# A small hybrid model on one core: the second layer's ternary maps, weight parts and softplus made inside the layer ahead of it

## What is computed

```python
# chosen-token layer: 128 tokens of highest score go through attention and a gated MLP
x1 = x + attn_out
h2 = rms_norm(x1, ln2_w)
mlp = silu(h2 @ w_gate) * (h2 @ w_up) @ w_down
...
# layer 1, gated recurrence along the tokens
gates, values = split(x @ W.T + b)
hidden = scan(sigmoid(gates), tanh(values))
...
# layer 1, ternary feed-forward (three maps of 1024 x 256)
scale = mean(abs(w)) + 1e-8
q = clip(round(w / scale), -1, 1) * scale
...
# layer 1, recurrent block
log_a = -8.0 * softplus(a_param) * sigmoid(x @ ga_W + ga_b)
```

## Time and profile before

| | |
|---|---|
| median of three runs | 1559.47 us (1554.13 to 1560.02) |
| the profiled execution, its time | 1559.31 us |
| its span | 1558.1 us |
| busy in the span | PE 94%, DVE 74%, ACT 66%, POOL 44% |
| TensorE's mean granted clock | 0.978 of full |
| f2: start, its `x1`, first addition to x | 1186.2, 1256.12, 1271.04 us |
| layer 1: first centring to the end | 1275.43 to 1558.1 us |

### The profile page before, as it was taken

The page is one execution under the profiler, slowest core; times in us unless marked ns, Lnnn a source line. Parts: engine busy times, 40 slices in busy tenths (PEclk is TensorE's granted clock), DMA queues, the critical chain, the costliest instruction groups (busy, mean ns, idle before and its releaser), DMA issues.

```text
span 1558.1 us, 23609 instructions
## 1 busy us (share of the span) xinstructions
PE 1461.4 (94%) x8358; PEld 1214.0 (78%) x8358; DVE 1145.6 (74%) x2617; ACT 1024.1 (66%) x2254; POOL 679.4 (44%) x802
## 2 busy tenths in 40 slices
PE   6999999999999998998999999999999987978898
PEld 4878888888888886686888888888886864655576
DVE  6888898989898985656675766766666748787646
ACT  3798989888888986453664655655654446464654
POOL 4557676665666554043433332333221411722233
PEclk8999999999999999998999999999999998998999
DMA  2000000000000000601000000000004122000000
GB/s 85 11 1 1 18 1 18 1 18 2 17 8 1 8 1 1 258 1 49 21 21 8 21 28 8 28 21 15 1 8 179 80 85 105 1 0 0 1 1 28
DMA packets 14341, 45.12 MB, mean 29 GB/s; under 512 B 3216, under 2 KB 3216, under 8 KB 12048
## 3 DMA queue, kind: packets, MB, share of 16 engines
q1 hardware_dynamic: 14224, 43.61, 7.9%
HBM read 42.55 MB, written 1.05 MB: 28 GB/s over the span
## 4 chain that ended last, share of the span: by engine, by line
PE 64%; DVE 16%; ACT 16%; issue 3%; POOL 1%; DMA 1%; SPq 0%; DVEq 0%; ACTq 0%; POOLq 0%
PE ps L148 26%; PE ps L345 13%; PE ps L1137 8%; PE ps L334 7%; ACT a_pT_hi L393 4%; ACT a_prob L361 3%; ACT a_o_two L634 3%; PE ps L1911 2%; DVE a_prob L354 2%; PE ps L1917 2%; DVE a_pT_lo L401 2%; ACT a_q L624 1%; DVE f_r L1527 1%; PE ps L1927 1%; PE ps L1913 1%
## 5 line engine op out<-in xcount | busy, mean ns | idle before, releaser
L376 POOL TENSOR_SCALAR a_prob<-a_prob,a_rowinv 128x128 f32<-128x128 f32 (+7 forms) x256 | 188.3, 750 | 164.2 <-DVE a_rowinv L370 164.2
L361 ACT ACTIVATE a_prob<-a_prob,a_negmax 128x128 f32<-128x128 f32 (+7 forms) x256 | 198.4, 780 | 32.5 <-DVE a_negmax L354 30.9
L401 DVE TENSOR_TENSOR a_pT_lo<-ps,a_pT_hi 128x512 fp32r<-128x512 f32 (+3 forms) x384 | 193.0, 549 | 19.9 <-ACT a_pT_hi L393 17.3
L376 POOL TENSOR_SCALAR b_prob<-b_prob,b_rowinv 128x128 f32<-128x128 f32 (+7 forms) x128 | 94.2, 748 | 234.6 <-DVE b_rowinv L370 234.6
L354 DVE CUSTOM_DVE_ANT_0 a_prob<-ps,a_mask 128x128 f32<-128x128 f32 (+7 forms) x256 | 187.2, 749 | 8.8 <-PE ps L148 8.4
L393 ACT ACTIVATE a_pT_hi<-ps 128x512 fp32r<-128x512 f32 (+3 forms) x384 | 164.2, 492 | 22.5 <-PE ps L334 9.9
L334 PE MATMUL ps<-ident,a_prob 128*128 128x128 f32 x1152 | 155.0, 275 | 8.8 <-DVE a_pT_lo L401 6.6
L361 ACT ACTIVATE b_prob<-b_prob,b_negmax 128x128 f32<-128x128 f32 (+7 forms) x128 | 99.7, 779 | 82.5 <-DVE b_negmax L354 82.3
L334 PEld LDWEIGHTS ps<-ident,a_prob 128*128 128x128 f32 x1152 | 128.9, 140 | 27.3 <-issue 11.2
L148 PE MATMUL ps<-a_k_hi,a_q 128*128 128x512 f32 (+3 forms) x384 | 141.0, 373 | 7.6 <-DVE a_negmax L354 7.5
L345 PE MATMUL ps<-a_pT_hi,a_v 128*128 128x512 f32 (+3 forms) x384 | 132.5, 352 | 1.6 <-DVE a_q L664 0.7
(11 more groups left out here) (449 smaller groups left out, 4145.1 us busy)
## 6 DMA issues: line engine op xcount, KB each, us to landing
f_wq<-in_f_wq SPq DMA_DIRECT2D x2, 2048.0 KB, 9.2
f_wo<-in_f_wo SPq DMA_DIRECT2D x2, 2048.0 KB, 17.5
b_w_raw<-in_b_qk SPq DMA_DIRECT2D x16, 256.0 KB, 2.6
a_w_raw<-in_a_w SPq DMA_DIRECT2D x8, 384.0 KB, 3.3
a_o_raw<-in_a_o SPq DMA_DIRECT2D x8, 256.0 KB, 2.7
f_wk<-in_f_wk SPq DMA_DIRECT2D x2, 1024.0 KB, 11.1
f_wv<-in_f_wv SPq DMA_DIRECT2D x2, 1024.0 KB, 13.1
f_wg<-in_f_wg SPq DMA_DIRECT2D x2, 1024.0 KB, 19.6
```

The costliest lines, as they stand in the source:

```text
L361: act.activation(prob, prob, ACT.Exp, bias=a.negmax[:, n:n + 1], scale=-1.0, accum_out=a.rowsum[:, n:n + 1]).then_inc(*g.exped.mark(a.tag, u))
L376: pool.tensor_scalar(prob, prob, a.rowinv[:, n:n + 1], 1.0, ALU.mult, ALU.mult).then_inc(*g.normed.mark(a.tag, u))
L401: dve.tensor_tensor(lo, src, fr(hi), ALU.subtract).then_inc(*g.lo.mark(a.tag, u, j0 // 4))
```

## The change

- In the layer f2 (`early=True`), layer 1's memory is laid out first, and tiles of `ffn` are put in another order, so that layer 1's early tiles lie on tiles of f2 that are dead by then (the rotary table, wq, wk, wv and two small masks).
- SP, at the end of f2's own loads, waits for `take` 7 and issues four small loads, then waits for the last query/key product and issues the three ternary weights and the recurrence's weights (`early_sp`). Layer 1's own list keeps the recurrent block's weights alone.
- The sum of absolute values moves from ACT to DVE (`early_abs_dve`, one `tensor_reduce` of 2048 columns), reading the same average matrix as the norms, with the factor 1/1024 in the scale. The three means on PE, the scales, five of the six half maps and the sixth in layer 1's first DVE step (`prep_dve`), the first half of the softplus and its Abs, Exp and Ln are put between f2's instructions. After the Ln ACT calls the root once (`warm_act`).
- POOL splits the recurrence's weights in f2, ahead of `ch` (`early_pool`).
- The four strings are written anew, for lists without most zeros. On POOL, the splits of layer 1's other weights stand at other places between the ring's low parts.

```diff
 def ffn_pool(g, f, pool):
...
             pool.tensor_tensor(g.x[:, k, cc], g.x[:, k, cc], f.h[:, k, cc], ALU.add).then_inc(*done.mark(tag, "x_plus", b, k))
+    if f.early:
+        early_pool(g, f.early, tag, pool)
     pool.wait_ge(*g.f_dve.at(tag, "x1"))
...
 def ffn_pe(g, f, pe):
...
     weigh(0)
+    if f.early:
+        early_pe(g, f.early, pe, 0, 3)
     turn_prob(2)
...
     weigh(3)
+    if f.early:
+        early_pe(g, f.early, pe, 1, 3)
     out(2)
...
     t.then_inc(*done.mark(tag, "chT"))
+    if f.early:
+        early_pe(g, f.early, pe, 2, 0)
     pe.wait_ge(*act.at(tag, "chT"))
...
 def ffn_act(g, f, act):
...
     weighed(2)
+    if f.early:
+        early_exp_act(g, f.early, act)
     weighed(3)
...
     act.activation(f.chT[:], bank[3][:, 0:D], ACT.Copy, scale=f.gate[:]).then_inc(*done.mark(tag, "chT"))
+    if f.early:
+        early_ln_act(g, f.early, act)
...
 def ffn_dve(g, f, dve):
...
     divide(2)
+    if f.early:
+        early_abs_dve(g, f.early, tag, dve, 0)
     divide(3)
+    if f.early:
+        dve.wait_ge(*pe.at(tag, "v", 1))
+        early_scale_dve(g, f.early, dve, 0, 3)
+        ternary_dve(g, f.early, dve, 0, 0)
+        early_abs_dve(g, f.early, tag, dve, 1)
+        ternary_dve(g, f.early, dve, 0, 1)
+        early_scale_dve(g, f.early, dve, 1, 3)
+        early_exp_dve(g, f.early, dve)
+        ternary_dve(g, f.early, dve, 1, 0)
     dve.wait_ge(*act.at(tag, "xs"))
     dve.wait_ge(*pe.at(tag, "wo"))
...
         dve.tensor_scalar(f.h2[:, k], f.x1[:, k], f.ln[:, 1, k:k + 1], None, ALU.mult).then_inc(*done.mark(tag, "h2", k))
+    if f.early:
+        ternary_dve(g, f.early, dve, 1, 1)
     dve.wait_ge(*act.at(tag, "root"))
...
+    if f.early:
+        early_abs_dve(g, f.early, tag, dve, 2)
+        early_scale_dve(g, f.early, dve, 2, 0)
+        ternary_dve(g, f.early, dve, 2, 0)
     for c, cc in halves():
         for m in range(KT):
             dve.wait_ge(*pe.at(tag, "put", m, c))
...
+def early_sp(g, l, tag, sp):
+    sp.wait_ge(*g.f_dve.at(tag, "take", TT - 1))
+    sp.dma_start(l.r_b[:], g.ins["r_b"]).then_inc(*g.r_loaded.mark("b", by=16))
...
+    sp.wait_ge(*g.f_pe.at(tag, "qk", len(F_ORDER) - 1))
+    for name, _, _ in TERNARY:
+        sp.dma_start(l.raw["t", name][:], g.ins["t_" + name]).then_inc(*g.t_loaded[name].mark(by=16))
+    sp.dma_start(l.raw_r[:], g.ins["r_w"]).then_inc(*g.r_loaded.mark("w", by=16))
+
+def early_pe(g, l, pe, n, bank):
+    pe.wait_ge(*g.prep_dve.at("abs", n))
+    pe.matmul(g.bank[bank][:, P + n * 32:P + n * 32 + 1], g.avg[:], l.part[:, n:n + 1], start=True, stop=True).then_inc(*g.prep_pe.mark("mean", n))
+
+def early_pool(g, l, tag, pool):
+    pool.wait_ge(*g.r_loaded.at("w"))
+    pool.wait_ge(*g.f_pe.at(tag, "v", 1))
+    split_in_place(pool, l.r_w, l.raw_r, g.prep_pool, "r")
+
+def early_abs_dve(g, l, tag, dve, n):
...
+    dve.tensor_reduce(l.part[:, n:n + 1], l.raw["t", name][:].rearrange(FLAT), AX.X, ALU.add,
+                      apply_absolute_value=True).then_inc(*g.prep_dve.mark("abs", n))
+
+def ternary_dve(g, l, dve, n, c):
...
+    dve.tensor_scalar(l.below[:, cc], raw[:, cc], s[:, 2:3], None, ALU.is_lt).then_inc(*g.prep_dve.mark("below", n, c))
+    dve.wait_ge(*g.prep_dve.at("below", n, c))
+    dve.scalar_tensor_tensor(w[:, cc], raw[:, cc], s[:, 1:2], l.below[:, cc], ALU.is_gt,
+                             ALU.subtract).then_inc(*g.prep_dve.mark("t", name, c))
```

## The result

The changed kernel is slower, by less than half a percent. Its eight runs have a median of 1563.63 us (1558.66 to 1565.48); the kernel before beside them 1559.54 (one of its eight took 6504.73, which leaves the median where it is); the ratio is 1.0038, with a 95% interval of 1.0021 to 1.0056. Two later sets gave 1.0070 (1.0046 to 1.0094) and 1.0053 (1.0033 to 1.0073). The forecast was 1551.4, faster, with a range of 1544.5 to 1559: wrong in size and in sign.

A forecast was written before the change was run, and what follows sets the result against it. The kernel was taken as bound by PE's matmuls, so gains lie only where PE waits, chiefly before 1330 us. Terms 3.3 + 1.7 + 1.1 - 5.5 - 5.9 - 2.6 = -7.9 gave 1551.4 us, range 1544.5 to 1559.

The forecast's parts named there:

- A: In f2, up to `x1`: DVE's added work and its waits on POOL's instructions make `x1` later, +3.3 us (+0.2 to +6.0).
- clock: At the MLP of f2: PE's idle 3.9 us before it lowers the granted clock behind it, +1.7 us (0 to 3.4).
- additions: From `x1` to the first centring: DVE's added sum, scale and half maps delay the additions and centring, +1.1 us (0 to 2).
- B: Centring to the first root: waiting for the load and ACT's table changes go, -5.5 us (-6.0 to -4).
- C: First normalised tokens to first "up" product: DVE is rid of comparisons, products and scales, -5.9 us (-9.9 to -3).
- D: "up" 0 to "up" 2 of half 0: no down map in front of `silu` on DVE, -2.6 us (-3.4 to -2.0).
- E: After 1330 us: new strings swap turns and POOL's splits move; no sign known, 0 (-3 to +4).
- The slower rival: After the opening: POOL's splits between ring parts delay PE's "down" products, +16.7 us, making 1568 us; chance 0.08.
- Taken back: After 1330 us: the halves wait for each other's scans and lose the opening's gain, 1555 to 1559 us; chance 0.09.
- signs of being wrong: Reduction far from 2.3 us, `x1` under 1257 or over 1262, "up" 2 after 1326, later PE waits over 32 or under 24.

The follow-up runs named there:

- e15: The changed kernel measured again unaltered, in five rounds: 1563.4 us, ratio 1.0053 to the kernel before.
- a1: The changed kernel measured once more unaltered, beside fresh runs of the kernel before: 1567.1 us, ratio 1.0070.
- e7: e2 with the down map's two halves moved on DVE into its waits ahead of half 0's scans: 1554.4 us, ratio 0.9991.
- e8: The changed kernel without POOL's splits of up2 and down, PE reading up1's parts instead, no turn moved: 1554.4 us, ratio 0.9972.
- e2: The changed kernel with all four engines' turns as in the kernel before, only the early work new: 1553.4 us, ratio 0.9987.
- e6: e4 with POOL's splits cut into pieces of 512 columns, one behind each ring part: 1553.6 us, ratio 0.9983.
- e4: The changed kernel with half 1's `silu` 6 and its product ahead of half 0's `b` on DVE: 1563.3 us, ratio 1.0031.
- e5: e2 with POOL's list alone exchanged for the changed kernel's: 1563.3 us, ratio 1.0044.
- e3: The changed kernel with all eight splits at the head of POOL's list: 1559.0 us, ratio 1.0007.
- e13: e2 measured again in five rounds: 1553.7 us, ratio 0.9978.
- e11: e9 with POOL's splits in pieces of 512 columns, as in e6: 1554.9 us, ratio 0.9971.
- e9: e7 with the split of the recurrence's weights after `x1` and the gate map's halves later on DVE: 1551.3 us, ratio 0.9953.
- e10: e6 with the same moves in f2 as e9: 1552.4 us, ratio 0.9954.

## Why the prediction was wrong, step by step

The marks of e15 against before, both from the last `divide`:

| stretch | forecast | measured |
|---|---|---|
| to `x1` (A) | +3.3 | +2.5 |
| `x1` to the first centring (clock, additions) | +2.8 | +2.7 |
| centring to the first tokens (B) | -5.5 | -3.7 |
| tokens to "up" 0 (C) | -5.9 | -5.8 |
| "up" 0 to "up" 2 (D) | -2.6 | -2.3 |
| "up" 2 to the end (E) | 0, -3 to +4 | +14.1 (first profile +10.8, a1 +11.8) |

A: the reduction is 2.27, as estimated from the product, and free of POOL, as the Trainium skill says on the page "SBUF — State Buffer", section "Who interferes with whom"; the trace agrees (2.27 beside `r_hi`, 2.28 with POOL idle). There were three meetings worth 1.0, 0.9 and 0.6 us; I had 3.1 in all. The clock: there in nine of the twelve profiles, absent in three (the change's first, a1, e7). B: I had counted 4.1 us from the first centring to the first root; it is 5.3 (1277.88 to 1283.13), since the first variance waits for three centrings, 1.9 us, and a product of the squares; another 0.5 lies between root and tokens. C and D: right as sized. At "up" 2 the five make -6.7 instead of -7.9.

**E is the step that failed: "The new strings swap single turns of the halves, and POOL's splits stand elsewhere. I know no sign for it: 0".** I had the sign in hand. In A I walked through DVE's instructions beside POOL's, one by one, because a split lay there; and in the rivals I named the same splits of up2 and down, at the same places in POOL's list, and asked only who is queued behind them on POOL. The question that I put in f2, which instruction of DVE runs beside this one and where are its operands, I did not put here. Answered, it puts `one_less` and the scan beside two low parts of 3.5 us each, in a chain for which PE waits: the 7.6 us above, and a sum near no change. E measured +10.8 to +14.1 in the three profiles of the change, and +1.4 in e8, where the two splits are away.

That would still not be slower. 2.9 more are `silu` behind the scan. The two lengthen PE's longest wait by 10.5 us; PE's other idle time behind "up" 2 is 1.4 less. The rest is PE's clock: the same matmuls there take 1.7 us more in the first profile and 4.3 more in e15, at a granted clock of 0.94 and 0.92 instead of 0.96. Over all executions of these kernels, the time of one kernel rises about 10 us for each 0.01 of its mean granted clock. The change has 0.974 over its three sets, the kernel before 0.979 beside the later two: some 5 us. Kernels without the long wait (e2, e6, e8) have 0.978 to 0.979. In 1380 to 1400, around the 13.8 us, the granted clock is 0.66, before 0.83. But the length of the longest wait does not sort the kernels alone: e4 and e5, with 7.3 us, have 0.975 like the change, and e3, with 6.2, has 0.978. That the long wait is what costs the clock is therefore likely and not shown. I had counted such a price for a wait of 3.9 us in f2, 1.7 us, and none for any wait later.

The slower rival (0.08) had the right sign and the right instructions, at 1568, and the wrong victim: it priced PE's "down" products behind POOL. In the change no row of PE waits for POOL. "Taken back" (0.09) is wrong as well: with the splits away the gain stays (e8), though e7 shows that a further 3 us at the first centring can vanish before the end. What I had named as signs of being wrong was met: PE was idle 36.5 us after 1330 (227.4 less 190.9), not 24 to 32.

With all turns as before nothing is lost behind the opening: e2 and e13 are 3.3 and 3.7 us ahead at "up" 2, and e13's time is 3.4 us under before. Not settled: which of the new turns of PE, DVE and ACT bring the 3 us more that the change has at "up" 2, what of them is left at the end, and what lowers the clock.

## What to carry to other kernels

When work moves to another place in one engine's list, ask two things of it there: who stands behind it on its own engine, and, between POOL and DVE, what runs beside it on the other, with the operands of each. In these runs an instruction of DVE that reads PSUM keeps its time beside POOL (0.65 to 0.75), and so does a reduction (2.27); the others with all operands in SBUF end only behind POOL's, so a long POOL instruction belongs beside a stretch of DVE that reads PSUM, and nowhere near a scan on the critical chain. Then ask whether PE waits for the instruction that is held up: the 7.6 us above cost time, the 2.7 of the two low parts did not. Cut a long instruction into pieces only where no such stretch is long enough (e11); and when PE's waits grow, look at the granted clock too.

## What the runs showed of the hardware

- What DVE loses goes by its operands and by the length of the one POOL instruction beside it, not by POOL's share of busy time. POOL at 19.3 of 20 us in pieces of 0.6 and 1.3 cost the readers of PSUM nothing (e6); POOL at 15.2 of 20, with pieces of 3.75 and 3.73 beside `one_less` and a scan, cost PE 7.6 us. The same `one_less` takes 3.81 beside 3.75 of POOL, 1.64 beside 1.71, and 0.69 alone.
- The loss is on both sides: `r_hi`, 1.04 alone, took 2.01 in f2 beside DVE's product, and a high part of 1536 columns 1.91 to 2.40 instead of 1.47.
- With the same program and the same wait the clock behind the MLP's wait was 1.00 in some executions and 0.87 in others: 3.4 us gave both (the change and e15, one program), and so did 1.56 (e9 and e10, the same f2). A term for the clock is a chance times a price, not a fixed cost.
